# A two-layer network on one Trainium2 core: convolution read from PSUM, first weight chunks of three stages reordered or joined, and zero products at twelve places

## What is computed

```
x = x + xattn0(norm(x), ctx)     # A: cross attention, 16 heads
x = x + attn0(norm(x))           # B: self attention with rotary angles
x = x + ffn0(norm(x))            # C: 6 gated + 2 shared experts, two passes
x = x + xattn1(norm(x), ctx)     # D: latent cross attention, 16 heads, key width 384
x = x + mixer1(norm(x))          # E: a Mamba-2 mixer, inner width 2048
x = x + ffn1(norm(x))            # F: 8 experts, top 2, with LoRA
```

```
xc = conv(hBC, conv_w, padding=3 on the left, one filter per channel)
hBC = silu(xc + conv_b);  xs, B, C = split(hBC)
y = scan(dt, xs, B, C) + D * xs
out = rmsnorm(y * silu(gate)) * norm_w @ W_out.T
```

## Time and profile before

| what | value |
|---|---|
| median of 3 runs | 1474.01 us |
| range of the runs | 1473.71 to 1476.0 us |
| the profiled execution's own time | 1474.45 us |
| its span in the profile | 1472.40 us |
| mean granted clock of PE | 0.989 |
| busy: PE | 1369.9 us, 93% of the span |
| busy: DVE | 1034.4 us, 70% |
| busy: POOL | 699.8 us, 48% |
| busy: ACT | 640.4 us, 43% |
| DMA | 87.94 MB, mean 60 GB/s |

### The profile page before, as it was taken

One profiled execution on the slowest core, in us unless ns is written; L12 is line 12 of the kernel. 1 busy time (PEld: TensorE's weight loads), 2 busy tenths in 40 slices (PEclk: granted clock), 3 DMA queues, 4 the chain that ended last, 5 costly groups with the idle time before them and its releaser, 6 DMA issues.

```text
span 1472.4 us, 24058 instructions
## 1 busy us (share of the span) xinstructions
PE 1369.9 (93%) x8806; PEld 1140.0 (77%) x8807; DVE 1034.4 (70%) x1552; ACT 640.4 (43%) x1339; POOL 699.8 (48%) x468
## 2 busy tenths in 40 slices
PE   7989899999989999799999999999999987979998
PEld 4667678678768787699899899999767766856886
DVE  5446675678678887577777777776448999846555
ACT  3524443353332323566566566665335455432000
POOL 3233477768647764431431331400555665525663
PEclk9999999999999999999999999999999999999999
DMA  4112123223242231000000001000231121212332
GB/s 142 57 37 66 58 86 94 88 77 93 72 150 81 90 87 43 24 25 24 2 24 24 2 24 35 19 1 1 67 105 58 59 71 58 65 43 79 95 90 71
DMA packets 31476, 87.94 MB, mean 60 GB/s; under 512 B 3472, under 2 KB 3600, under 8 KB 31120
## 3 DMA queue, kind: packets, MB, share of 16 engines
q1 hardware_dynamic: 31376, 86.53, 18.8%
HBM read 85.46 MB, written 1.05 MB: 59 GB/s over the span
## 4 chain that ended last, share of the span: by engine, by line
PE 65%; DVE 18%; ACT 8%; issue 7%; POOL 1%; DMA 0%; ACTq 0%; DVEq 0%; POOLq 0%
PE psum L816 19%; PE psum L818 18%; PE psum L817 18%; DVE conv_acc L2536 5%; PE psum L1308 3%; DVE part_max L2420 3%; ACT expo L1817 2%; ACT expo L1822 2%; ACT expo_t L1829 2%; PE psum L839 1%; PE psum L847 1%; DVE decay_in L2573 1%; DVE sq_sum L2649 1%; DVE expo_t L2023 1%; DVE psum L2607 1%
## 5 line engine op out<-in xcount | busy, mean ns | idle before, releaser
L636 POOL TENSOR_SCALAR wpair<-landing 128x1024 fp32r<-128x1024 f32 (+3 forms) x120 | 113.5, 946 | 414.9 <-PE psum L818 316.7
L639 POOL TENSOR_TENSOR wpair<-landing,wpair 128x1024 fp32r<-128x1024 f32 (+3 forms) x120 | 252.7, 2106 | 10.0
L816 PE MATMUL psum<-xn,wpair 128*128 128x512 f32 (+1 forms) x556 | 213.3, 384 | 5.7 <-POOL wpair L639 4.1
L817 PE MATMUL psum<-xn,wpair 128*128 128x512 f32 (+1 forms) x556 | 208.7, 375 | 0.0
L818 PE MATMUL psum<-xn,wpair 128*128 128x512 f32 (+1 forms) x556 | 208.6, 375 | 0.0
L2023 DVE TENSOR_TENSOR expo_t<-psum,expo_t 128x512 fp32r<-128x512 f32 (+1 forms) x224 | 143.6, 651 | 79.9 <-ACT expo_t L1829 78.1
L1829 ACT CAST expo_t<-psum 128x512 fp32r<-128x512 f32 (+1 forms) x224 | 124.2, 564 | 130.2 <-PE psum L1308 129.4
L816 PE MATMUL psum<-expo_t,kv_pair 128*128 128x256 f32 (+1 forms) x416 | 134.1, 322 | 4.1 <-DVE expo_t L2023 4.1
L1308 PE MATMUL psum<-const,expo 128*128 128x128 f32 (+1 forms) x832 | 127.5, 273 | 5.1 <-DVE kv_t L2023 4.4
L2420 DVE TENSOR_REDUCE part_max<-psum 128x1 f32<-128x804 f32 x128 | 122.9, 987 | 12.6 <-PE psum L818 10.6
L816 PEld LDWEIGHTS psum<-xn,wpair 128*128 128x128 f32 x556 | 104.5, 188 | 30.2 <-POOL wpair L639 4.8
(11 more groups left out here) (310 smaller groups left out, 3383.0 us busy)
## 6 DMA issues: line engine op xcount, KB each, us to landing
landing<-in_weights SPq DMA_DIRECT2D x71, 512.0 KB, 3.6
landing<-in_weights SPq DMA_DIRECT2D x97, 256.0 KB, 2.6
kv<-in_ctx SPq DMA_DIRECT2D x8, 832.0 KB, 4.5
landing<-in_weights SPq DMA_DIRECT2D x16, 384.0 KB, 3.1
landing<-in_weights SPq DMA_DIRECT2D x15, 320.0 KB, 2.9
rope_k<-in_rope_k SPq DMA_DIRECT2D x1, 1664.0 KB, 7.2
const<-in_constants SPq DMA_DIRECT2D x1, 1184.0 KB, 8.9
x<-in_x SPq DMA_DIRECT2D x4, 256.0 KB, 4.2
```

The costliest lines, as they stand in the source:

```text
L636: pool.tensor_scalar(wpair[:, slot, 0, 0:width], landing[:, slot, 0:width], 1.0, 1.0, ALU.mult, ALU.mult).then_inc(chunk_high, 1)
L639: pool.tensor_tensor(wpair[:, slot, 1, 0:width], landing[:, slot, 0:width], wpair[:, slot, 0, 0:width].bitcast(F32), ALU.subtract).then_in ...
L816: pe.matmul(out, w(0), act(0), start=start, stop=False)
L817: pe.matmul(out, w(0), act(1), start=False, stop=False)
```

## The change

1. **Chunks of B joined.** The first tiles of q and k, and every later pair, share a chunk of 1024 columns. A new semaphore `q_done` says when q's half is done. V's chunks are BB + 1 and BB + 2.
2. **C, first pass:** the chunk of expert 1's first up tile moves ahead of expert 0's second chunk; the tile is computed into bank 7 (`EARLY_BANK`) before `second_products(0, 0)`.
3. **F:** LoRA's chunk becomes the third. `normal_tiles` takes the router and Wg of expert 0; Wu follows, then the LoRA product into bank 7, whose copy ACT makes behind the silu of expert 0.
4. **Zero products** (`keep_going`): products of zeros in bf16, 128 x 512, whose results nobody reads. Six ahead of each half's square sums in norms 1 to 5, eight ahead of the wait in `value_latents(0)`, seven ahead of the last `down`.
5. **E:** `conv_in`, its memset and ACT's 18 copies go. DVE's steps read the PSUM bank, shifted by 3, 2 and 1 tokens, and leave out the columns in front (61, 62 and 63 of 64 tokens of each batch). B and C go to banks 4 and 5. PE's `inner_tiles(i)` now waits for DVE's last step on the bank, and DVE does both convolutions one after the other, ahead of `inner_by_dt`.

In the diff, lines with "..." stand for parts left out (semaphore declarations, the indices of chunks that shift by the new order, the wait of ACT's copies on them).

```diff
-            ("B", (half, half, CHUNK, CHUNK), 1), ("B", (half, half), FT - 1), ("B", (CHUNK, CHUNK), 1)]
+            ("B", (CHUNK,) * (FT + 4), 1)]
...
-             ("F", (half,) + (CHUNK,) * 5 + (half,), 1), ("F", (CHUNK,) * 6, 3), ("F", (CHUNK,), 1)]
+             ("F", (CHUNK, CHUNK, half, CHUNK, CHUNK, CHUNK, half), 1), ("F", (CHUNK,) * 6, 3), ("F", (CHUNK,), 1)]
...
-        for o in (0, FT):
-            chunk(*[tile(w, k, o + f) for k in range(FT)])
+        chunk(*[tile(w, k, o + f) for o in (0, FT) for k in range(FT)])
...
-    for _ in range(2):
+    for p in range(2):
         up_c(0)
+        if p == 0:
+            up_c(1, (0,))
         sw_c(0)
-        up_c(1)
+        up_c(1, (0, 1) if p else (1,))
...
-    chunk(*[tile(lora_a, k, 0) for k in range(FT)])
     wide = lambda w: chunk(*[tile(w, k, m) for m in range(2) for k in range(FT)])
     deep = lambda w: chunk(*[tile(w, k, m) for m in range(FT) for k in range(2)])
     for e in range(2):
         wide(i["L1_ffn_Wg"][e])
         wide(i["L1_ffn_Wu"][e])
+        if e == 0:
+            chunk(*[tile(lora_a, k, 0) for k in range(FT)])
...
-            conv_in = sb("conv_in", [P, 2, B, S + CONV_K - 1], F32, scope)
...
+        def conv_bank(v, m):
+
+            return m if v else 4 + m
...
+            def keep_going(k_bank, products):
+
+                for _ in range(products):
+                    pe.matmul(bank(k_bank), zero_b[:, 0:P], zero_b[:, :], start=True, stop=True)
...
+                    if k:
+                        keep_going(LN_BANKS[k][1 + half], 6)
...
-                slot = BB % 2
-                chunk_ready(BB + 1)
-                normal_tiles(1, [(bank(0), slot_tile(slot, 0), chunk_used), (bank(1), slot_tile(1 - slot, 0), chunk_used)])
+                chunk_ready(BB)
+                normal_tiles(1, [(bank(0), slot_tile(BB % 2, 0), q_done), (bank(1), slot_tile(BB % 2, FT), chunk_used)])
...
-                    for side in range(2):
-                        project(BB + 4 + 2 * f + side, (slot, 1 - slot)[side], side)
+                    n = b_chunk(f + 1)
+                    chunk_ready(n)
+                    wide(n % 2, 0, xn, bank(0)).then_inc(q_done, 1)
+                    wide(n % 2, FT, xn, bank(1)).then_inc(chunk_used, 1)
...
+                    up_tile(0, 1, 0, EARLY_BANK)
                 second_products(p, 0)
                 turn_logits(p)
-                up_tiles(p, 1)
+                if p:
+                    up_tile(p, 1, 0)
+                up_tile(p, 1, 1)
...
+                    keep_going(2, waiting)
...
-                value_latents(0, D3B % 2, 0).then_inc(chunk_used, 1)
+                value_latents(0, D3B % 2, 0, 8).then_inc(chunk_used, 1)
...
-                    pe.wait_ge(xs_copied, 2 * i + 2)
-                    pe.wait_ge(conv_last, 2 * i + 2)
-                    two_tiles(EB + 1 + 2 * i, (EB + 1) % 2, xn, 0, xs_done)
+                    chunk_ready(EB + 1 + 2 * i)
+                    for m in range(2):
+                        if i:
+                            pe.wait_ge(conv_step, 6 * i + 3 * m + 3)
+                        wide((EB + 1) % 2, FT * m, xn, bank(conv_bank(i + 1, m))).then_inc(chunk_used if m else xs_done, 1)
...
-                for n in (FB, FB + 1):
-                    chunk_ready(n)
-                normal_tiles(5, [(bank(4)[0:NE, :], gate_tile(2), logits), (bank(7), slot_tile(FB % 2, 0), chunk_used),
-                                 (bank(0), slot_tile((FB + 1) % 2, 0), first),
-                                 (bank(1), slot_tile((FB + 1) % 2, FT), chunk_used)])
+                chunk_ready(FB)
+                normal_tiles(5, [(bank(4)[0:NE, :], gate_tile(2), logits), (bank(0), slot_tile(FB % 2, 0), first),
+                                 (bank(1), slot_tile(FB % 2, FT), chunk_used)])
+                chunk_ready(FB + 1)
+                wide((FB + 1) % 2, 0, xn, bank(2)).then_inc(second, 1)
+                turn_logits(2)
+                wide((FB + 1) % 2, FT, xn, bank(3)).then_inc(chunk_used, 1)
                 chunk_ready(FB + 2)
-                wide(FB % 2, 0, xn, bank(2)).then_inc(second, 1)
-                turn_logits(2)
-                wide(FB % 2, FT, xn, bank(3)).then_inc(chunk_used, 1)
+                wide(FB % 2, 0, xn, bank(7)).then_inc(chunk_used, 1)
...
+                pe.wait_ge(silu_done, 2 * 3 * NE)
+                keep_going(0, 7)
...
-                            act.wait_ge(conv_step, 6 * v + 3 * m - 3)
-                        act.copy(conv_in[:, m, :, CONV_K - 1:], by_batch(bank(m))).then_inc(xs_copied, 1)
-                        if v:
                             act.wait_ge(conv_silu, 2 * v + m - 1)
                         w = CONV_K * (tile + m) + CONV_K - 1
-                        act.activation(conv_acc[:, m, :], bank(m), ACT.Identity, bias=conv_b[:, tile + m:tile + m + 1],
+                        act.activation(conv_acc[:, m, :], bank(conv_bank(v, m)), ACT.Identity, bias=conv_b[:, tile + m:tile + m + 1],
...
-                act.wait_ge(chunk_used, FB + 1)
-                act.copy(lora_h[:, :], bank(7)).then_inc(lora_in, 1)
...
+                act.wait_ge(chunk_used, FB + 3)
+                act.copy(lora_h[:, :], bank(7)).then_inc(lora_in, 1)
...
-                dve.memset(conv_in[:, :, :, 0:CONV_K - 1], 0.0).then_inc(conv_pad, 1)
...
-                        dve.scalar_tensor_tensor(out=acc, in0=conv_in[:, m, :, t:t + S], scalar=conv_w[:, w:w + 1],
-                                                 in1=acc, op0=ALU.mult, op1=ALU.add).then_inc(conv_step, 1)
+                        late = CONV_K - 1 - t
+                        dve.scalar_tensor_tensor(out=acc[:, :, late:], in0=by_batch(bank(conv_bank(v, m)))[:, :, 0:S - late],
+                                                 scalar=conv_w[:, w:w + 1], in1=acc[:, :, late:], op0=ALU.mult, op1=ALU.add
+                                                 ).then_inc(conv_step, 1)
...
+                    convolve(i + 1, 2 * i, 1)
                     inner_by_dt(i - 1)
                     mixes(i - 1)
-                    convolve(i + 1, 2 * i, 1)
```

More of the change, by code:

```diff
@@ L751, in perceiver_stack @@
         GATE_0 = (0, 15, 30)
+        EARLY_BANK = 7
         C_SPREAD_BANKS = (5, 6, 4, 7, 5, 6)
@@ L768, in up_chunk @@
             base = CB + C_CHUNKS * p
+            if p == 0 and e == 1 and m == 0:
+                return base + 2
             return base + (m if e == 0 else 3 + m if e == 1 else 5 + 2 * m if e == 2 else 5 * e - 4 + m)
@@ L1039, in _ @@
                     for g in range(G):
-                        mm = all_values((BB + c) % 2, g, lambda part, k: xn[:, part, k, :], 2, 2 * c, c == 1, 3)
+                        mm = all_values((BB + 1 + c) % 2, g, lambda part, k: xn[:, part, k, :], 2, 2 * c, c == 1, 3)
                         if c == 1 and g < G - 1:
@@ L1128, in up_tile @@
                         pe.wait_ge(second_low, k + 1)
-                    mm = product(bank(m), quarter_tile(n, k), tokens(xn, k), start=k == 0, stop=k == FT - 1)
+                    mm = product(bank(k_bank), quarter_tile(n, k), tokens(xn, k), start=k == 0, stop=k == FT - 1)
                 mm.then_inc(chunk_used, 1)
@@ L1393, in _, with value_latents @@
                 units(B // 2 - 1, True)
-                def value_latents(h, slot, buffer):
+                def value_latents(h, slot, buffer, waiting=0):
                     chunk_ready(D3B + h)
+                    keep_going(2, waiting)
                     pe.wait_ge(ctx_low, h + 1)
@@ L1432, in _ @@
                 chunk_ready(EB)
-                normal_tiles(4, [(bank(0), slot_tile(EB % 2, 0), bc_done), (bank(1), slot_tile(EB % 2, FT), chunk_used)])
+                normal_tiles(4, [(bank(conv_bank(0, 0)), slot_tile(EB % 2, 0), bc_done),
+                                 (bank(conv_bank(0, 1)), slot_tile(EB % 2, FT), chunk_used)])
                 dt_w = small_at("dt_w").rearrange("p (k h) -> p k h", h=MH)
@@ L1525, in output_chunk @@
                     if c == 0:
-                        pe.wait_ge(xs_copied, IT + 2)
-                        pe.wait_ge(conv_last, IT + 2)
+                        pe.wait_ge(conv_step, 3 * IT + 6)
                         pe.wait_ge(gate_silu, IT)
@@ L1719, in hidden_in @@
                     bias = small_at("c_up_bias")[:, 2 * e + m:2 * e + m + 1]
-                    act.activation(hid[:, e % 2, m, :], bank(m), ACT.Identity, bias=bias).then_inc(hid_in, 1)
-                    act.activation(hid_pair[:, 0, m, :], bank(m), ACT.Identity, bias=bias).then_inc(hid_high, 1)
+                    k_bank = EARLY_BANK if p == 0 and e == 1 and m == 0 else m
+                    act.activation(hid[:, e % 2, m, :], bank(k_bank), ACT.Identity, bias=bias).then_inc(hid_in, 1)
+                    act.activation(hid_pair[:, 0, m, :], bank(k_bank), ACT.Identity, bias=bias).then_inc(hid_high, 1)
             def silus(p, e):
```

23 lines of the change are left out of this document (13 added, 10 removed).

## The result

The changed kernel takes 1440.06 us (median of 4 runs, 1438.08 to 1442.9) against 1475.01 for the kernel before: ratio 0.9762, 95% interval 0.9737 to 0.9787. In a second group of runs it took 1441.62 against 1474.04 (0.9767, 0.9738 to 0.9797). The forecast was 1443.7, range 1437 to 1454.

A forecast was written before the change was run, and what follows sets the result against it. PE, busy 93% of the span, bounds the kernel, but DVE paces the mixer loop. Terms 5.2 + 0 + 3.0 + 0 + 3.6 + 14.8 + 5.9 - 1.7 = 30.8 off 1474.45 give 1443.7 us, range 1437 to 1454.

The forecast's parts named there:

- E, 20.7: Mixer stage: convolution steps reading PSUM take 0.75 us, so PE becomes the bound; loop and tail save 20.7 us.
- the loop with what lies ahead of it: Mixer loop: PE's waits for DVE in the loop and 1.56 us ahead of it go; 14.8 us saved.
- the tail: End of the mixer: 3.1 us of PE idle time and half the low-clock time go; 5.9 us saved.
- B, 5.2: Stage B: joined chunks remove the hole before the first value products and the low clock behind it; 5.2 us saved.
- Norms' and last down's zero products, 0: Norms and last down product: zero products fit in existing holes, with the norms' clock already at 1.00; 0 us gained.
- C, 0 and its charge: Stage C: the early up tile only moves the hole, 0 us; 1.7 us charged for one clock drop at remaining holes.
- F, 3.6: Stage F: LoRA's chunk third lets the fourth chunk's split start and be ready earlier; 3.6 us saved.
- D3, 3.0: Start of D3: eight zero products in a 2.38 us hole hold the clock up; 3.0 us saved.
- (a): Mixer rival: convolution steps only partly quicker, 1.35 us, as POOL may still disturb them; whole 1453.9 us; chance 0.14.
- (b): Mixer rival: PSUM reads cost what the copies saved, steps 1.49 us or more, no gain there; whole 1464.4; chance 0.05.
- (c): Mixer rival: PE waits for DVE's last step on each bank, making it slower; 1489 to 1518 us; chance 0.03.
- (d): Norms rival: zero products at the low clock end up to 1 us late ten times; whole 1453.7 us; chance 0.05.

The follow-up runs named there:

- the kernel before with narrow zeros: Sixty zero products of 16 columns added in the norms of the kernel before, nothing else changed: 1468.59 us, ratio 0.9949.

## Why the prediction was right

It was right in the time and in its largest terms, and partly by luck in the sum: in the profiled pair D gave 4.4 us more than its term, and E and F together gave 3.4 less.

- **E, 20.7:** measured 20.66 alone. In the changed kernel the loop with what lies ahead of it gave 14.6 (forecast 14.8), the tail 5.9 (5.9). What came on top was a clock drop at E's start, behind 32 narrow products in which PE doesn't stand at all: 1.6 us in the profiled execution, in no term.
- **B, 5.2:** 5.18. **Norms' and last down's zero products, 0:** the square sums of norm 4 to the first product behind them take 5.21 us in both kernels; a zero product costs 0.215 (eight in 1.90, the last one's end included).
- **C, 0 and its charge:** the hole moved as forecast, +1.77 in the profiled execution.
- **F, 3.6:** too large by 1.0. The step that failed is the ready time of the fourth chunk. Counted from the norm's first square sums, POOL should have begun its split at 19.7 us, 3.4 us before 23.1. It began at 20.4 and took 3.7, its first half 1.23 instead of 1.04, beside DVE's gate operations.

```profile
1296.20 1.23 POOL L638 TENSOR_SCALAR wpair<-landing 128x1024 fp32r<-128x1024 f32 x1 [4.14 <-issue]
1297.51 2.37 POOL L641 TENSOR_TENSOR wpair<-landing,wpair 128x1024 fp32r<-128x1024 f32 x1
```

- **D3, 3.0:** the amount came (2.9), but in the changed kernel not by the step named, "by holding the clock": it stays up without the products too. They may have done it at the old moment, as the run without the norms' zero products suggests. And what it won came back in part as the drop at E's start.
- **Missing: 6.2 us in D's loop.** The prediction asked what the zero products do to PE's time and clock, never what sixty more instructions do to the place of all code behind them. The trace before has the idle time, 1.94 us at 717.7 and 1.93 at 827.0, 109 us apart, and I took it for part of the units' pace. In the profiled pair 3.9 us were taken back by a low clock for 17 us at the start of the units. Another 2.2 were won: about 1.6 by two clock drops that only the trace before has, of 3.4 us each and directly behind the two stalls (719.1 and 828.3), the rest by a wait for DVE of 0.80 at 929.33 that the changed kernel doesn't have. The prediction's reason for D3, that the clock reads 1.00 in the kernel's other stretches of steady products, passed over these drops.

Rivals: (a), (b) and (c) hung on the steps' price, which was 0.73 with or without POOL. PE never waits on `conv_step` in the loop. (d) needed a low clock in norms 1 to 5, which no profile of the changed kernel shows; the kernel before with narrow zeros has one, for 3.4 us from 1292.1, in the norm of F.

## What to carry to other kernels

Where DVE sets the pace beside a busy POOL, look at the spread of one operation's durations before its mean: a fast mode, and slow ones that end at a fixed distance behind POOL's operations, point to the second SBUF input as the cost, and here reading that input from PSUM was worth more than a copy. In a kernel with a long loop on an engine, look for idle time where the loop turns back, look at how long the branch there takes, and count the instruction loads; inserting or removing instructions far ahead can be worth more than what they do. And judge a clock drop over several executions: filling C's hole removed the drop behind it and nothing from the time.

## What was unexpected of the hardware

- A loop of PE that turns back can cost 3.1 us (a branch of 3.6 to 3.8 us, 17 more instruction loads for two turns) or nothing (a branch of 0.2), by 36 products more or fewer ahead of it.
- An operation of DVE with two SBUF inputs ended 0.53 to 0.55 us after POOL's in all 35 cases in which it was held up.
- The same 2.38 us hole was followed by 6.8 us at the lower clock in five kernels and by none in two.
- The clock fell in E at 1102.42 while PE was busy all through, in 32 products of 32 columns; the same products had 1.00 in the kernel before. The profiles have this drop just where they lack the one in D3.
- Executions of one kernel differ by more than their profiles suggest: 1470.3 to 1481.3 us for the kernel before in one group of 19, with mean granted clocks of 0.982 to 0.991.
